# Two places in the beat of a tiled attention: sums against first scores on TensorE, the context's norm against the row maxima on VectorE

## The reference

```python
def _mha(x, y, ...):
    xn = _ln(x, lnx_g, lnx_b)
    yn = _ln(y, lny_g, lny_b)
    q = einsum('bsc,hcd->bhsd', xn, wq)
    k = einsum('btc,hcd->bhtd', yn, wk)
    v = einsum('btc,hcd->bhtd', yn, wv)
    a = softmax(einsum('bhsd,bhtd->bhst', q, k) * D ** -0.5)
    if causal:
        a = a * mask
    o = einsum('bhst,bhtd->bhsd', a, v).reshape(...)
    x_out = x + o @ li1_w + li1_b
    h = gelu(_ln(x_out, ln3_g, ln3_b) @ li2_w + li2_b)
    return x_out + h @ li3_w + li3_b
x = _ln(x, ln1_g, ln1_b)
x = x + _mha(x, x, ..., causal=True)
x = _ln(x, ln2_g, ln2_b)
return x + _mha(x, ee, ..., causal=False)
```

## Time and profile before

| | us |
|---|---|
| median of 3 runs | 3585.2 |
| lowest, highest | 3582.9, 3586.72 |
| the profiled execution | 3584.1 |
| its span | 3582.3 |
| PE busy | 3274.7 (91%) |
| DVE busy | 2394.3 (67%) |
| ACT busy | 1978.5 (55%) |
| POOL busy | 2059.3 (57%) |

### The profile page before, as it was taken

How to read it: one execution, slowest core, us unless ns; L and a number is a source line. 1 busy time by engine, 2 the same in 40 slices (tenths; PEclk the granted TensorE clock), 3 DMA queues, 4 the chain that set the end, 5 groups by cost and what they waited for, 6 DMA issues and landing times. The chain is left out here.

```text
span 3582.3 us, 99654 instructions
## 1 busy us (share of the span) xinstructions
PE 3274.7 (91%) x39893; PEld 2049.4 (57%) x39893; DVE 2394.3 (67%) x5651; ACT 1978.5 (55%) x3574; POOL 2059.3 (57%) x1842
## 2 busy tenths in 40 slices
PE   6999999998899999898999999998999989999686
PEld 3554554454455555565666666775555545666575
DVE  5888888886455555476555555876777765666465
ACT  5666666663556666442566554435666646666354
POOL 4778877886577878664111112646777752433365
PEclk8999999999999999998999999999999999999798
DMA  4222222222900000000000000000000000000364
GB/s 140 87 88 89 89 86 88 81 84 99 316 23 2 2 2 2 16 1 12 4 5 5 5 4 6 1 8 8 2 2 2 2 16 18 26 17 15 90 175 118
DMA packets 50273, 164.52 MB, mean 46 GB/s; under 512 B 11823, under 2 KB 23218, under 8 KB 40785
## 3 DMA queue, kind: packets, MB, share of 16 engines
q1 hardware_dynamic: 45520, 150.43, 12.8%
q0 software_dynamic: 4352, 8.47, 0.7%
HBM read 149.89 MB, written 43.65 MB: 54 GB/s over the span
## 5 line engine op out<-in xcount | busy, mean ns | idle before, releaser
L504 DVE TENSOR_TENSOR_SCAN XC<-ssm_dA,ssm_db 128x2048 f32<-128x2048 f32 x128 | 565.4, 4418 | 110.0 <-PE ssm_db L359 97.4
L567 POOL TENSOR_TENSOR XC<-XC,XB 128x1536 f32<-128x1536 f32 x128 | 505.7, 3951 | 180.8 <-DVE XC L504 134.4
L373 PE MATMUL ssm_y<-XC,weights 128*128 128x512 f32 x1024 | 472.3, 604 | 2.5 <-POOL XC L567 2.3
L453 ACT ACTIVATE ssm_dA<-ssm_delta,ssm_nega 128x508 f32<-128x508 f32 x512 | 325.2, 707 | 84.1 <-DVE XC L504 83.6
L1193 POOL TENSOR_TENSOR self_pm<-self_pT,weights 128x512 f32<-128x512 f32 x256 | 322.9, 1298 | 63.1 <-ACT self_pT L922 61.6
L373 PEld LDWEIGHTS ssm_y<-XC,weights 128*128 128x128 f32 x1024 | 187.6, 191 | 215.6 <-issue 204.2
L1199 POOL TENSOR_TENSOR XC<-XC,XB 128x128 f32<-128x128 f32 x128 | 58.7, 459 | 400.1 <-DVE XB L1076 400.1
L2628 POOL TENSOR_TENSOR XC<-XC,weights 128x512 f32<-128x512 f32 x128 | 161.6, 1284 | 95.8 <-ACT XC L2462 95.8
L1062 DVE TENSOR_REDUCE self_nmax<-self_scores 128x4 f32<-128x512 f32 x256 | 158.4, 680 | 86.9 <-PE self_scores L802 86.9
L359 PEld LDWEIGHTS ssm_db<-XB,ssm_dxT 32*128 32x128 f32 x4096 | 135.9, 189 | 99.2 <-DVE XC L504 64.9
L359 PE MATMUL ssm_db<-XB,ssm_dxT 32*128 32x128 f32 x4096 | 161.7, 287 | 25.5 <-DVE XC L504 23.9
(11 more groups left out here) (450 smaller groups left out, 8179.7 us busy)
## 6 DMA issues: line engine op xcount, KB each, us to landing
XB<-c_rows SPq DMA_DIRECT2D x64, 1024.0 KB
sorted<-in_padding SPq DMA_DIRECT2D x1, 33280.0 KB, 111.3
experts_we<-in_w_experts SPq DMA_DIRECT2D x72, 323.0 KB, 3.5
experts_rt<-sorted SPq DMA_DIRECT2D x72, 65.0 KB
ssm_xT<-in_xT SPq DMA_DIRECT2D x16, 256.0 KB
XC<-in_w_experts SPq DMA_DIRECT2D x9, 256.0 KB
weights<-in_w_self SPq DMA_DIRECT2D x1, 1412.0 KB, 7.2
cross_ctx_t<-in_ctx SPq DMA_DIRECT2D x16, 77.0 KB
```

The source lines that it names most:

```text
L373: mm = pe.matmul(yp[half][:, :].rearrange("p (b t) -> p b t", b=GROUP), ident, of_state(states(32, at), k), start=(k == 0 and nq == 0 and ...
L453: o = act.activation(dA[:, p % 2, :].rearrange("p (b k t) -> p b k t", b=GROUP, k=4)[:, :, k, 1:T], by_batch(delta[:, slot, half, :])[:, : ...
L504: dve.tensor_tensor_scan(states(0, p).rearrange("p m t -> p (m t)"), dA[:, p % 2, :], db[:, :], 0.0, ALU.mult, ALU.add).then_inc(h_ready, 1)
L567: pool.tensor_tensor(states(32, p).rearrange("p (b k) t -> p b k t", k=4)[:, :, 0:3, :], states(0, p).rearrange("p (b k) t -> p b k t", k= ...
```

## The change

Two places in wide_attention_phase. In the self attention, in beats with t % 4 == 0, TensorE issues first_scores(t + 1) ahead of sums(t - 3) instead of behind it. In the cross attention, in beats with t % 4 == 3, VectorE applies the context's norm (ctx_norm) at the end of the beat, after the copy of the value job, instead of behind row_norm and ahead of maxima(t + 1). All waits and instructions stay the same.

```diff
--- before.py
+++ after.py
@@ -670,6 +670,7 @@
         VEC = 4 * GROUP
         POOL = 9 if own else 4
         BEATS = range(-1, N + 5)
+        SUMS_BEHIND = (0,) if own else ()
 
         def there(n):
             return 0 <= n < N
@@ -874,10 +875,13 @@
                 for g, n in early_jobs(t):
                     if (g, n) not in FRONT:
                         job(g, n)
-                if there(t - 3):
+                behind = t % GROUP in SUMS_BEHIND
+                if there(t - 3) and not behind:
                     sums(t - 3)
                 if there(t + 1):
                     first_scores(t + 1)
+                if there(t - 3) and behind:
+                    sums(t - 3)
                 if there(t - 3):
                     weighted(t - 3)
                 if there(t):
@@ -1044,7 +1048,11 @@
                         in_stats(g)
                     if not own and p == 3:
                         row_norm(g)
-                        ctx_norm(g)
+
+            def late_norms(t):
+                g, p = t // GROUP + 2, t % GROUP
+                if not own and g < NG and p == 3:
+                    ctx_norm(g)
 
             def split(n):
                 dve.wait_ge(max_ready, 4 * n + 4)
@@ -1117,6 +1125,7 @@
                     scaled(t - 3)
                 for g, n in late_jobs(t):
                     empty(g, n)
+                late_norms(t)
 
         @block.gpsimd
         def _(pool):
```

## The result

The changed kernel takes 3574.2 us as the median of 7 runs (3563.1 to 3576.0); the kernel before takes 3586.7 us in the runs beside it (7 runs, 3582.9 to 3590.2). The ratio of the two is 0.9957, with a 95% interval of 0.9944 to 0.9971: faster by 15 us, between 10 and 20. The forecast was 3569.1 us in a range of 3564.0 to 3577.5. The sum of 16.1 us lies inside the interval of the ratio. The distance between the two medians, 12.5 us, is less than that; single runs of one kernel lie up to 13 us apart here.

A forecast was written before the change was run, and what follows sets the result against it. The prediction took a round closed by VectorE's late maxima to bound both attentions. Gains of 5.8 us (self) and 10.3 us (cross) sum to 16.1, so 3585.2 - 16.1 = 3569.1 us, range 3564 to 3577.5.

The forecast's parts named there:

- The sum of 16.1 us: Both attentions together: 5.8 us from the self attention plus 10.3 from the cross attention, bounds 13.7 to 17.5.
- What bounds the kernel: Both attentions: a round of first scores, maxima, second scores and exponential, which late maxima on VectorE delay.
- The self attention, 5.8 us: First beats of a group: maxima start 0.29 us earlier in 13 beats, 1.00 us in two; bounds 3.9 to 5.8.
- The fourth selector, 0.37 - 0.29 = 0.08 us: Self attention's first beat: the last selector matmul's wait for the maxima shrinks from 0.37 to 0.08 us.
- The late logarithm, at nothing: Self attention's first beat: sums come 1.10 us later, their logarithm on ScalarE ends at 1035.16, costing nothing.
- The cover of 0.28 us: Self attention's first beat: time between the logarithm's end, 1035.16, and the turn matmul waiting for it, 1035.44.
- The rival of the late turn: Self attention's 15 first beats: the turn waits for the logarithm, making the kernel slower, 3593.7 us; chance 0.03.
- the first rival: Self attention: the swap gives nothing, only the cross attention's 10.3 us stands, 3574.9 us; chance 0.12.
- The cross attention, 10.3 us: Last beat of a group: interval between first scores falls from 8.42 to 7.63 us, 0.79 in 13 groups.
- The norm at its new place, at nothing: Cross attention's beat end: the norm's 0.90 us fits in VectorE's 1.23 us of idle time, with 0.92 behind.
- The bound that gave the norm 0.87 us for a meeting with GpSimd: Cross attention: at most, the moved norm is lengthened by 0.87 us to 1.77, with the next maxima still not late.
- The rival by which the gain is handed back a beat later: Cross attention: the moved norm makes the next maxima late, only the self attention's 5.8 us stands, 3579.4 us; chance 0.07.

The follow-up runs named there:

- statistics late: The changed kernel with the self attention's statistics of x also moved behind the row maxima, to the first beat's end: 3563.3 us, 0.9929 of the kernel before.
- row norm late: The changed kernel with the cross attention's row norm also moved to the end of the beat, ahead of the context's norm: 3571.0 us, 0.9945 of the kernel before.
- swap alone: The changed kernel with the context's norm put back, so only the self attention's order of sums and first scores differs from before: 3581.0 us, ratio 0.9975.
- context alone: The changed kernel with the self attention's swap taken out, so only the context's norm is moved: 3577.6 us, 0.9971 of the kernel before.
- before again: The kernel before, unedited, run once more for a second profile: 3592.5 us.
- norm three times: The changed kernel with the context's norm made three times at its new place, twice into an unread tile, from the third group: 3576.2 us, ratio 0.9951.

## Why the prediction was right

**What bounds the kernel.** Right in both phases: the chain of first scores, maxima, second scores and exponential sets the interval. Maxima that come earlier shorten it where a selector waits for them (statistics late), and do nothing where none waits (row norm late).

**The self attention, 5.8 us.** Measured 5.7 in the profile. The step was 0.29 us in 13 beats and 1.00 in two. Measured are 9.30 + 7.46 - 8.30 - 8.14 = 0.32 in each of the 13, and 1.00 in each of the two. 13 x 0.32 + 2.00 = 6.2; the beat with the stall gained 0.55 instead of 1.00, which leaves 5.7. That 5.7 comes so near to the forecast's 5.8 is luck in part: each of the 13 beats gave a little more than 0.29, and without the stall the 6.2 would lie above the upper bound of 5.8. What the prediction took from the third beat, a first reduction 0.09 us ahead of the aggregates' end, is 0.08 here. Statistics late showed the reason, VectorE; the 0.68 us that it returned are the part of the 1.00 that the prediction rightly kept out of its sum.

**The fourth selector, 0.37 - 0.29 = 0.08 us.** Wrong: it waits 0.38 us. The step looked at the last wait alone. In the same beat of before, two selectors waited, as the timeline of TensorE has it:

```profile
1036.59 0.23 PE L824 MATMUL self_scores<-self_nmT,self_pick 32*128 32x128 bf16 x1 [0.31 <-DVE self_nmax L1062]
1037.18 0.23 PE L824 MATMUL self_scores<-self_nmT,self_pick 32*128 32x128 bf16 x1 [0.37 <-DVE self_nmax L1062]
```

Each waits for its own reduction, and the reductions come some 0.6 us apart in both kernels (2.48 us for four in before, 2.45 in after). Maxima that start 0.28 us earlier took the third selector's wait away and left the fourth's. The gain of the interval comes out the same, since the fourth starts 0.31 us earlier against the first of the pair (1035.04 - 1030.50 = 4.54 us, before 1037.18 - 1032.33 = 4.85).

**The late logarithm, at nothing.** Right. The cover of 0.28 us is 1033.48 - 1033.34 = 0.14 us in fact, since the shorter order brings the turn 0.13 us nearer to the first of the pair (2.98 us, before 3.11), and it holds: the turn has no idle time in front. The rival of the late turn (3593.7 us) is out, as is the first rival, under which the swap gives nothing: swap alone is faster by 4.7 us at the least.

**The cross attention, 10.3 us.** Measured 13 x 0.79 = 10.3 in the beats and 10.4 (5.4 to 15.4) by context alone. The interval in the first group was the right measure of what is left when the maxima are in time: the new interval is the same 7.63 to the hundredth, although the row norm still takes 1.98 us beside GpSimd's residual.

**The norm at its new place, at nothing.** Right, but by more than the working had it. It left 1.23 - 0.9 = 0.33 us and then 0.92. Measured are 0.54 and 0.92. What was mis-sized is the add, put 0.4 us late: it stands 1869.91 - 1868.21 = 1.70 us ahead of the next first scores, where it stood 1882.36 - 1880.45 = 1.91 us ahead, so it is 0.21 us late. Two things make the difference. In before the split, the step ahead of the add, starts like this:

```profile
1879.59 0.15 DVE L1053 CAST cross_nsplit<-cross_nmax 128x16 bf16<-128x16 f32 x1
```

That is 1882.36 - 1879.59 = 2.77 us ahead of the next first scores, and 1869.91 - 1867.93 = 1.98 in the kernel after, so VectorE's queue is 0.79 us late against TensorE, the low end of 0.8 to 0.9. And the add, which no longer waits, starts 0.09 us before the split's end (1868.12 + 0.18 = 1868.30). 0.79 - 0.50 - 0.09 = 0.20 us. The bound that gave the norm 0.87 us for a meeting with GpSimd was not needed. The row norm takes 1.98 us beside the residual and 1.11 or 1.10 (row norm late) without it, and the context's norm takes 0.96 us at its new place, where it meets nothing. What makes the row norm longer beside the residual no run shows. The rival by which the gain is handed back a beat later is out: 6.38 us, unchanged.

**The time.** The sum was 16.1 us, and the changed phases gave 15.9. The measured median lies 5.1 us above the forecast, inside the range: 1.5 us because the kernel before had a median of 3586.7 and not 3585.2 us in the runs beside it, and 3.6 us because the medians lie 12.5 us apart and not 16.1. The profiled execution lost 9.1 us in the narrow phase, which the change doesn't touch; that this phase varies by as much without the change is shown by the kernel before, 387.2 and 398.0 us in two executions. That the 3.6 us come from this is likely and not shown: the runs of before that go with this result have no clock on record, and it would take profiles of many executions. What is shown is that time and granted clock go together from run to run in context alone and in the 23 runs of before. So the mechanisms and the sum of the beats were right, and how near the median came is in part luck. The prediction allowed 1 to 2 us for run to run, which was too little; runs of one kernel lie up to 20 us apart (the kernel before, 3580.6 to 3600.2), and it was the bounds and the first rival that made the range wide enough.

## What to carry to other kernels

In a round of engines that wait for each other, the worth of an earlier step is read from what the engine behind it did just before, and where the same phase has a beat in which the step happens to be in time, that beat's interval is the measure to take: here it was right to 0.01 us (7.63). Where a group of waits is paced by several instructions of another engine, look at all of them, not at the last. When a swap makes one engine early and the other one's queue becomes the limit, look at what stands in that queue ahead of the step: here moving it was worth more in the beats (8.8 us) than the swap (5.7).

## What the runs showed of the hardware

- The granted clock at the start of the narrow phase differed between two executions of the kernel before, and the phase took 387.2 and 398.0 us. In the kernel after it was at 0.50 from 2912.6 to 2919.4 us and again from 2926.2 to 2953.5 us; TensorE was busy for 6.2 and 7.6 of 10 us in the two windows from 2910 to 2930 us and for 9.3 and 9.9 in the next two. With idle time filled it kept 1.00 in one profile (2910 to 2940 us) and fell in another, at 2923.7 and 2930.6 us, where TensorE was busy for 8.0 and 9.1 of 10 us in the windows from 2910 and 2920 us and, in the 15 us up to the first fall, idle for at most 0.97 us at a time; why is open. The kernels before and after had nearly the same idle stretches there, the longest 4.12 us in both; the clock of the first was at 0.50 there for 6.8 us, that of the second for 6.8 and then 27.3 us.
- The granted clock changed between 1.00 and 0.50 on a grid of 3.4133 us, within 0.03 us, in each of the twelve profiles (31 to 41 changes from 60 to 3560 us). The grid's first point after the span's start lay between 0.10 us (row norm late) and 3.36 us (context alone); it was the same to 0.01 us in one pair of profiles (0.58, before again and norm three times).
- Executions of one program can differ in the mean granted clock, and the time with it: the twelve runs of context alone fall into 3574.5 to 3578.0 us at 0.972 to 0.977 and 3586.9 to 3588.6 us at 0.968 to 0.972.
- The stall without a releaser in the self attention's beat 8 makes its interval 11.7 to 15.4 us long, against 8.3 to 9.3 in the beats like it, and is not tied to the edit: two profiles of before have 15.4 and 12.7. An interval of 11.16 us instead of 7.63 stands once in the cross attention too, after its first group's last beat, in the profile of statistics late. The cause of either is open.
- VectorE instructions that follow each other without a wait overlap by 0.07 to 0.09 us in the beats read here (maxima on aggregates, 1032.53 against 1032.61; the norm's 1.85 us for eight instructions that take 1.78 of the queue). Between the last statistics and the first aggregate stand 0.15 us of idle time, in the kernels before and after (1032.23).
- The eight sum matmuls and the 32 first scores take a little less in one order than in the other: 1032.49 - 1030.50 = 1.99 us up to the weighted outputs with the scores first, 2.10 us with the sums first (1034.43 - 1032.33 in the kernel before).
